# Layer 1's cross-attention with an input shift on GpSimd, scores ahead of a transpose and a mix smoothed by ScalarE, and layer 3's experts in column groups

## The reference, cut to what matters

```python
# L1_xattn
y = jnp.clip(x / scale, -448, 448).astype(bfloat16)    # _div_clamp_fp8, then
y = y.astype(float8_e4m3fn).astype(float32)            # rounded to 8 bits
ln_out = _ln(hidden_states, ln_w, ln_b)
q  = _ln(_fp8_linear_pertensor(ln_out, wq, ...))       # likewise k, qx; v without _ln
core = softmax(q k^T / sqrt(d)) v                      # xout: qx with kx, vx of cond
cat  = concatenate([core, xout])
catq = _div_clamp_fp8(cat, proj_smooth)                # a scale for each column
return (catq @ wproj) * (proj_in_scale * proj_w_scale)
# L3_ffn: 32 experts, at most 32 tokens each, F = 176
g = silu(einsum('ech,ehf->ecf', xe, Wg))
u = einsum('ech,ehf->ecf', xe, Wu)
ye = einsum('ecf,efh->ech', g * u, Wd)
```

## Time and profile before

| what | value |
|---|---|
| time of three runs, us | 3984.92 median, 3978.76 to 3985.75 |
| profiled execution, us | 3986.08, its span 3984.3 |
| PE busy | 3303.0 us, 83% of the span |
| PE weight loads | 2369.1 us, 59% |
| DVE busy | 2550.1 us, 64% |
| ACT busy | 1598.0 us, 40% |
| POOL busy | 301.1 us, 8% |

### The profile page before, as it was taken

How to read it: one execution, slowest core, us unless ns; L and a number is a source line. 1 busy time by engine, 2 the same in 40 slices (tenths; PEclk the granted TensorE clock), 3 DMA queues, 4 the chain that set the end, 5 groups by cost and what they waited for, 6 DMA issues and landing times. The chain is left out here.

```text
span 3984.3 us, 77894 instructions
## 1 busy us (share of the span) xinstructions
PE 3303.0 (83%) x28864; PEld 2369.1 (59%) x28864; DVE 2550.1 (64%) x6580; ACT 1598.0 (40%) x3845; POOL 301.1 (8%) x321
## 2 busy tenths in 40 slices
PE   7899999544687988988989883879977898778899
PEld 6565665211564656656556561658877776645788
DVE  6555555688686777767767767768871487475133
ACT  2244444477243555555555551334332344210011
POOL 3000000000330101101011010001000000000000
PEclk9899999655797999999999995988779999888699
DMA  2000000000400000000000003000000000150100
GB/s 93 29 22 16 22 22 7 1 0 0 144 11 4 1 1 3 1 3 1 1 3 1 1 2 91 1 8 14 16 6 0 1 0 1 36 145 26 39 11 11
DMA packets 89575, 79.10 MB, mean 20 GB/s; under 512 B 16640, under 2 KB 82752, under 8 KB 88896
## 3 DMA queue, kind: packets, MB, share of 16 engines
q1 hardware_dynamic: 88208, 75.57, 6.4%
q10 hardware_dynamic: 1200, 1.11, 0.1%
HBM read 74.57 MB, written 2.10 MB: 19 GB/s over the span
## 5 line engine op out<-in xcount | busy, mean ns | idle before, releaser
L3116 PE MATMUL bank<-L1w_w,L1x_xqT 128*128 128x512 f32 x640 | 303.6, 598 | 2.1 <-DVE L1x_xqT L3360 2.1
L1046 DVE TENSOR_REDUCE L0x_top<-bank 128x4 f32<-128x512 f32 x256 | 159.3, 684 | 105.1 <-PE bank L972 102.0
L1031 ACT ACTIVATE L0x_P<-bank,L0x_level 128x512 f32<-128x512 f32 x256 | 155.1, 688 | 157.1 <-PE bank L992 157.1
L3366 DVE TENSOR_REDUCE L1x_ssq<-L1x_square 128x4 f32<-128x512 f32 x192 | 131.6, 685 | 133.9 <-ACT L1x_square L3243 125.7
L3330 POOL TENSOR_TENSOR L1x_square<-L1x_square,L1x_total 128x512 f32<-128x512 f32 x128 | 133.2, 1041 | 1073.4 <-DVE L1x_total L3395 1073.4
L3265 ACT ACTIVATE L1x_square<-bank,L1x_top 128x128 f32<-128x128 f32 x512 | 182.0, 376 | 19.7 <-DVE L1x_top L3389 19.7
L3177 PE MATMUL bank<-L1w_wp,L1x_catb 128*128 128x256 bf16 x1536 | 188.4, 273 | 0.3 <-DVE L1x_catb L3351 0.3
L3243 ACT ACTIVATE L1x_square<-bank 128x512 f32<-128x512 f32 x192 | 114.9, 599 | 164.4 <-PE bank L3116 164.4
L3116 PEld LDWEIGHTS bank<-L1w_w,L1x_xqT 128*128 128x128 f32 x640 | 115.3, 192 | 99.4 <-issue 91.6
L888 DVE TENSOR_TENSOR x_sb<-x_sb,bank 128x256 f32 (+1 forms) x112 | 47.0, 420 | 197.3 <-PE bank L208 187.5
L3177 PEld LDWEIGHTS bank<-L1w_wp,L1x_catb 128*128 128x128 bf16 x1536 | 150.2, 98 | 35.4 <-issue 17.1
(11 more groups left out here) (650 smaller groups left out, 7915.8 us busy)
## 6 DMA issues: line engine op xcount, KB each, us to landing
L0x_mask<-in_maskrows SPq DMA_DIRECT2D x16, 512.0 KB, 3.3
L3w_wg<-in_L_ffn_Wg SPq DMA_DIRECT2D x8, 704.0 KB, 8.2
L3w_wu<-in_L_ffn_Wu SPq DMA_DIRECT2D x8, 704.0 KB, 9.7
L1a_wp_quarter<-in_L_xattn_wproj SPq DMA_DIRECT2D x4, 1024.0 KB, 6.1
L3x_ctxT<-in_ctxT SPq DMA_DIRECT2D x32, 128.0 KB, 2.1
L3w_wd<-in_L_ffn_Wd SPq DMA_DIRECT2D x8, 512.0 KB, 8.7
L0x_ctxT<-in_ctxT SPq DMA_DIRECT2D x16, 128.0 KB, 2.9
L1w_w<-in_L_xattn_wq SPq DMA_DIRECT2D x1, 2048.0 KB, 10.4
```

The costliest lines, as they stand in the source:

```text
L1031: act.activation(self.P[:, i % 2, r, :], self.work_bank[r][:, :], ACT.Exp, bias=self.level[:, :]).then_inc(self.p_ready.sem, 1)
L1046: dve.tensor_reduce(self.top[:, s, 16 * c + 4 * r:16 * c + 4 * r + 4], self.work_bank[r][:, :].rearrange("p (h k) -> p h k", h=4), X, ALU.max,
L3116: last = pe.matmul(made_bank[n % 4][:, :], inputs(SOURCE[n], k), w[:, k, 4 * n:4 * n + 4, :], start=(k == 0), stop=(k == C - 1))
```

## The change

The input's shift by `lnb` and its product with `in_inv` go from DVE to POOL, and the product `y4` is 16 bits wide. On PE, make_v(3) and score(0) stand ahead of flip(9); on ACT, exponentials(0) stand behind turn_hat(9) and exponentials(1) behind turn_hat(10). DVE's scale_out is gone: ACT's new `smooth_out(m)`, four activations with a scale column from PSUM to 16 bits in `yc`, stands behind the copy of turn_p(m+1), and `quantize(m)` clips `yc` in place. In the experts `hidden` holds the 32 tokens of an expert still in one of four column groups and moves its 352 columns of `Wg` and `Wu`; `turn` transposes the product back; `ye` is copied by DVE.

```diff
@@ L1_xattn, PE
+                pe.wait_ge(v_ready.sem, v_ready.after(b, 1))
+                make_v(3)
+                score(0)
                 flip(NG - 3)
-                score(0)
                 score(1)
                 flip(NG - 2)
                 flip(NG - 1)
-                pe.wait_ge(v_ready.sem, v_ready.after(b, 1))
-                make_v(3)
@@ ACT
+                def smooth_out(m):
+                    act.wait_ge(mixed.sem, mixed.after(b, m + 1))
+                    if m >= 2:
+                        act.wait_ge(cat_ready.sem, cat_ready.after(b, m - 1))
+                    for j in range(4):
+                        last = act.activation(yc[:, (m % 2) * 512 + j * 128:(m % 2) * 512 + (j + 1) * 128], mix_bank[m % 2][:, j * 128:(j + 1) * 128],
+                                              ACT.Copy, scale=smooth[:, 4 * m + j:4 * m + j + 1])
+                    last.then_inc(o_read.sem, 1)
...
                 for m in range(MG):
                     if m + 1 < MG:
                         turn_p(m + 1)
+                    smooth_out(m)
                     if m + 3 < MG:
                         exponentials(m + 3)
@@ POOL
+            def shift_x(b):
+                pool.wait_ge(x_scaled.sem, x_scaled.after(b))
+                step(pool.tensor_tensor(kit.xn[:, :], kit.xn[:, :], lnb[:, :], ALU.add))
+                pool.tensor_tensor(y4, kit.xn[:, :].unsqueeze(1).to_broadcast([128, 4, D]), in_inv[:, :, :],
+                                   ALU.mult).then_inc(y4_ready.sem, 1)
@@ DVE
-                step(dve.tensor_tensor(kit.xn[:, :], kit.xn[:, :], lnb[:, :], ALU.add))
-                step(dve.tensor_tensor(y4, kit.xn[:, :].unsqueeze(1).to_broadcast([128, 4, D]), in_inv[:, :, :], ALU.mult))
...
+                def quantize(m):
+                    smoothed = yc[:, (m % 2) * 512:(m % 2) * 512 + 512]
                     dve.wait_ge(o_read.sem, o_read.after(b, m + 1))
-                    step(dve.tensor_scalar(yc[:, 0:512], cat[:, :], E4M3_TOP, -E4M3_TOP, ALU.min, ALU.max))
+                    step(dve.tensor_scalar(smoothed, smoothed, E4M3_TOP, -E4M3_TOP, ALU.min, ALU.max))
...
                     if m + 1 < MG:
                         invert(m + 1)
-                    scale_out(m)
                     if m + 3 < MG:
                         maxima(m + 3)
@@ L3_ffn, PE
+                    for k in range(C):
+                        for j in range(PER):
+                            at = (g * PER + j) * CAP
+                            last = pe.matmul(hidden_bank[g % 2][j * CAP:(j + 1) * CAP, 0:2 * F], xeT[:, k, at:at + CAP],
+                                             wgu[:, g % SLOTS, j, k, :, :].rearrange("p n f -> p (n f)"),
+                                             start=(k == 0), stop=(k == C - 1), tile_position=(0, j * CAP))
...
+                hidden(0)
+                hidden(1)
+                for g in range(GROUPS):
+                    turn(g)
+                    if g + 2 < GROUPS:
+                        hidden(g + 2)
+                    down(g)
```

More of the change, by code:

```diff
@@ L3286, in batch @@
                 turn_hat(NG - 3)
+                exponentials(0)
                 turn_hat(NG - 2)
-                exponentials(0)
+                exponentials(1)
                 turn_hat(NG - 1)
-                exponentials(1)
                 keep_v(3)
@@ L3325, in _, with share @@
         def _(pool):
-            with pool.Fori(0, B) as b:
+            step = Steps(pool, pool_own)
+            def shift_x(b):
[3 more added lines that the diff above has]
+                                   ALU.mult).then_inc(y4_ready.sem, 1)
+            def share(b, m):
+                pool.wait_ge(inv_ready.sem, inv_ready.after(b, m + 1))
+                rows = P[:, m % 3, :].rearrange("p (h k) -> p h k", h=4)
+                pool.tensor_tensor(rows, rows, total[:, 4 * m:4 * m + 4].unsqueeze(2).to_broadcast([128, 4, 128]),
+                                   ALU.mult).then_inc(shared.sem, 1)
+            step.restart()
+            shift_x(0)
+            with pool.Fori(0, B - 1) as b:
+                step.restart()
+                shift_x(b + 1)
                 for m in range(MG):
[L3328 to L3331, removed]
+                    share(b, m)
+            for m in range(MG):
+                share(B - 1, m)
         @block.vector
@@ L3341, in scale_x, with to_e4m3, from_clipped @@
                     step(norm_vector(kit, dve, b, kit.xn[:, :]))
-                step(dve.scalar_tensor_tensor(kit.xn[:, :], kit.xn[:, :], rms[:, bass.ds(b, 1)], lnw[:, :], ALU.mult, ALU.mult))
-                step(dve.tensor_tensor(kit.xn[:, :], kit.xn[:, :], lnb[:, :], ALU.add))
-                step(dve.tensor_tensor(y4, kit.xn[:, :].unsqueeze(1).to_broadcast([128, 4, D]), in_inv[:, :, :], ALU.mult))
[L3346 to L3351, removed]
+                dve.scalar_tensor_tensor(kit.xn[:, :], kit.xn[:, :], rms[:, bass.ds(b, 1)], lnw[:, :], ALU.mult, ALU.mult).then_inc(x_scaled.sem, 1)
+            def to_e4m3(out, wide, n):
+                step(dve.tensor_scalar(yc[:, 0:n], wide, E4M3_TOP, -E4M3_TOP, ALU.min, ALU.max))
+                return from_clipped(out, yc[:, 0:n], n)
+            def from_clipped(out, clipped, n):
+                power, both = grid[:, 0:n], sums[:, 0:n]
+                step(dve.tensor_scalar(power.bitcast(U16), clipped.bitcast(U16), 0x7F80, None, ALU.bitwise_and))
+                step(dve.tensor_scalar(power.bitcast(U16), power.bitcast(U16), E4M3_LOW_BITS, E4M3_GRID_BITS, ALU.max, ALU.add))
+                step(dve.tensor_tensor(both, clipped, power, ALU.add))
+                return dve.tensor_tensor(out, both, power, ALU.subtract)
             def round_x(b):
-                step(dve.tensor_scalar(yc[:, 0:4 * D], flat(y4), E4M3_TOP, -E4M3_TOP, ALU.min, ALU.max))
-                from_clipped(flat(yb[:, :, :]), 4 * D).then_inc(xq_ready.sem, 1)
+                dve.wait_ge(y4_ready.sem, y4_ready.after(b))
+                to_e4m3(flat(yb[:, :, :]), flat(y4), 4 * D).then_inc(xq_ready.sem, 1)
                 dve.wait_ge(xq_ready.sem, xq_ready.after(b))
@@ L3395, in invert @@
                     dve.reciprocal(part, part).then_inc(inv_ready.sem, 1)
[L3397 to L3400, removed]
+                def quantize(m):
+                    smoothed = yc[:, (m % 2) * 512:(m % 2) * 512 + 512]
                     dve.wait_ge(o_read.sem, o_read.after(b, m + 1))
-                    step(dve.tensor_scalar(yc[:, 0:512], cat[:, :], E4M3_TOP, -E4M3_TOP, ALU.min, ALU.max))
-                def quantize(m):
+                    step(dve.tensor_scalar(smoothed, smoothed, E4M3_TOP, -E4M3_TOP, ALU.min, ALU.max))
                     if m >= 3:
                         dve.wait_ge(left.sem, left.after(b, m - 2))
-                    from_clipped(catb[:, m % 3, :], 512).then_inc(cat_ready.sem, 1)
+                    from_clipped(catb[:, m % 3, :], smoothed, 512).then_inc(cat_ready.sem, 1)
                     dve.wait_ge(cat_ready.sem, cat_ready.after(b, m + 1))
@@ L3487, in L3_ffn @@
         SLOTS = GROUPS - 1
-        wg, wu = (wx.sb(n, [128, SLOTS, PER, C, F]) for n in ("wg", "wu"))
+        wgu = wx.sb("wgu", [128, SLOTS, PER, C, 2, F])
         wd0, wd1 = wx.sb("wd0", [128, SLOTS, PER, D]), wx.sb("wd1", [128, SLOTS, PER, D])
@@ L3674, in hidden, with turn, down @@
                         pe.wait_ge(gu_ready, g - 1)
[L3675 to L3682, removed]
-                    last.then_inc(made, 1)
[L3685 to L3689, removed]
-                    pe.wait_ge(gu_ready, g + 1)
+                    for k in range(C):
[4 more added lines that the diff above has]
+                                             start=(k == 0), stop=(k == C - 1), tile_position=(0, j * CAP))
+                    last.then_inc(made, 1)
+                def turn(g):
+                    pe.wait_ge(gu_ready, g + 1)
+                    if g >= 2:
+                        pe.wait_ge(guT_ready, g - 1)
+                    turn_tensor(kit, pe, turn_bank[g % 2], gu[:, g % 2, :], 2).then_inc(gu_turned, 1)
+                def down(g):
+                    pe.wait_ge(guT_ready, g + 1)
                     if g >= 2:
@@ L3704, in silu @@
                         act.wait_ge(gu_ready, g - 1)
-                    act.activation(act_g[:, g % 2, 0, :], hidden_bank[g % 2][:, 0:128], ACT.Silu)
-                    act.activation(act_g[0:F1, g % 2, 1, :], hidden_bank[g % 2][0:F1, 128:256], ACT.Silu).then_inc(silu_ready, 1)
+                    act.activation(act_g[:, g % 2, :], hidden_bank[g % 2][:, 0:F], ACT.Silu).then_inc(silu_ready, 1)
                 silu(0)
@@ L3711, in _, with multiply @@
                         silu(g + 1)
-                    act.wait_ge(out_made, g + 1)
-                    act.copy(ye[:, g, :], out_bank[g % 2][:, 0:D]).then_inc(out_ready, 1)
+                    act.wait_ge(gu_turned, g + 1)
+                    if g >= 2:
+                        act.wait_ge(out_made, g - 1)
```

(15 more changed lines are left out.)

25 lines of the change are left out of this document (14 added, 11 removed).

## The result

The changed kernel takes 4050.96 us (median of four runs, 4049.22 to 4054.72) against 3982.24 before: ratio 1.0174, 95% interval 1.0156 to 1.0191. It is slower by some 69 us; the forecast was 4045 us. The profiled execution took 4054.72 us.

What follows compares the result with a forecast made beforehand. No engine alone bound cross-attention, with DVE and PE nearly full in the mix loop; PE bound the experts. 3986.1 +116.5 +10.6 −67 = 4046.2, less 1.2 to the median: 4045 us, range 4008 to 4090.

Steps and rivals of the forecast that it cites:

- Circle: Mix loop: invert(m+1), share, turn_p, copy, smooth_out(m), quantize(m), invert(m+2) wait in a ring; turn 3.74 to 5.55 us, +10.9 a batch.
- Scores in front: Batch head: make_v(3) fills PE's wait before flip(9), so turn_x and what follows come earlier, −1.9 us a batch.
- The sum: Whole kernel: 3986.1 us profiled, +116.5 cross-attention, +10.6 clock, −67 experts, giving 4046.2; 1.2 above the median, so 4045.
- Input shift: Batch input: POOL's add and product, 2.7 us, stay hidden before DVE's clip; PE waits less, −0.4 us a batch.
- the first shift: Before the batch loop: the first batch's shift on POOL is not hidden, +1 us once.
- End of the batch: From invert(7) to the next flip(0): late quantizations hide under PE's leftover work, 11.5 us for 12.99, −1.5 a batch.
- Batch without loss on the circle: One cross-attention loop batch before any clock loss: 10.9−1.9−1.5−0.4 = +7.1 us, +106.5 for 15.
- Clock: Mix loop: PE idles about 1.9 us a turn, so its clock may halve on turn_p; +10.6 us taken, bounds 0 and +42.
- the rival: Mix loop: the clock falls in every turn, +42 in place of +10.6 us, 4076 us; chance 0.13.
- the quarter: Mix loop: share taken of the +42 us bound for half clock on turn_p in every turn, +10.6 us.
- Last batch: Final cross-attention batch: no end-of-batch gain, so 10.9−1.9 = +9 us.
- Experts: Layer 3 experts: wide column passes and the clock rising to full take 24.5 us in place of 91.5, −67.

Runs made afterwards that it cites:

- runs 1 and 2: Changed kernel with one move each: smooth_out(m) ahead of the copy of turn_p(m+1) on ACT, 3876.9 us; invert(m+2) ahead of quantize(m) on DVE, 3851.2 us.
- run 3: Changed kernel with the four smoothing activations replaced by one copy, leaving out the column scales: 3985.6 us.
- run 5: Kernel before with only the mix smoothed by ScalarE, at the same queue places as in the change: 4143.6 us, ratio 1.0394.
- run 7: Kernel before with only make_v(3) and score(0) ahead of flip(9) and the exponentials moved accordingly: 3965.1 us, ratio 0.9949.
- run 8: Kernel before with only the input's shift on GpSimd, 16 bits: 3971.8 us, ratio 0.9962.
- Run 6: Kernel before with only the experts in column groups: 3914.2 us, ratio 0.9825.

## Why the prediction was right, step by step

- **Circle.** Right as to mechanism, order and size: 5.61 us a turn for 5.55 predicted. Every link came out within 0.05 us of the row from which it was taken; the four activations took 1.15 us (1.14 taken). My estimate of 1.27 us from the Trainium skill's figures ("ScalarE: Activation LUTs", section on what ACT_TABLE_LOAD costs) is 0.12 more than this trace shows. Cutting either of two links (runs 1 and 2) or shortening one (run 3) moved the time as a circle must. Six turns are 33.95 us for 33.3, 0.06 more in each and 0.28 more in the first (5.89), and against 22.55 before +11.4 a batch, not +10.9. Not foreseen was the first turn: it is the scores in front that lengthen it, as run 5 without them has 5.60.
- **Scores in front.** −2.0 for −1.9 where it was looked for, and flip(9) no longer waits. The sum let everything behind turn_x keep its order and come 1.9 us earlier; it left out that the copy of turn_p(0) then waits for ACT's own queue. That gives back 0.58 a batch alone (run 7) and 0.28 in the changed kernel, whose circle hides the rest. That a half-clock stretch comes to more of the heads with this part alone (12 of 15 instead of 8) was not in the sum either.
- **Input shift.** Hidden as predicted: add and product took 0.73 and 2.36 us on POOL, in place of 0.8, which was an estimate without a row, and the 1.9 of the row; the product ended at 1423.79, the clip began at 1425.58. −0.28 a batch (run 8) for −0.4; the first shift +1.2 for +1.
- **End of the batch.** −1.6 for −1.5 (run 5); from invert(7) to flip(0) 11.39 us for 11.5 predicted (1398.99 to 1410.38).
- **Batch without loss on the circle.** 11.1 (run 5) −2.0 (run 7) −0.28 (run 8) −1.6 (run 5) +0.28 (the first turn, which only the parts together have) = +7.5, and 79.50−71.97 is +7.5, for the +7.1 of the sum.
- **Clock.** Right as to mechanism, in part luck as to size. Stretches at the half clock lengthen the heads of the 15 batches of the loop, from invert(0) to invert(2), by 10.7 us in all; in the kernel before it was 10.2, so nothing is new there. New are 6.2 us in the later turns: where the clock falls on turn_p the turn is up to 6.08 us, 0.46 more, as the rival said of each turn; but that meets single turns. With 1.3 us in the last batch it is some 8 us, for 10.6 predicted; the quarter was a choice, not a reading. The shown turn has leave at half speed (2.64 us for 1.47), and its length is still 5.62: there a low clock off the path cost nothing.
- **Last batch.** From its invert(0) to its last leave 47.87 us for 34.56, +13.3 where the sum has +10.9 (the −1.9 in its +9 lies ahead of that invert(0)): mis-sized by 2.4. Its six turns took 35.29 us, two of them 6.07 and 6.08 with turn_p at half speed.
- **Experts.** 23.2 us for 24.5; a turn was 2.55 for 2.65, and the clock was at the half level only for the first 3.4 us (mean 0.93 over the window of 24 us), so it rose during the hidden projections. The prediction's reading that it rises in the down projections was weak: before, it rose once, behind the fourth of them (3717.2), and not behind the three ahead of it. Run 6 gives the part alone as 70 by the ratio, 74 by the medians.
- **The total.** 4051 is 6 us above 4045. Against the profiled execution, 4054.7 us for the sum's 4046.2, 8.5 are missing: the cross-attention +131.5 for +126.1 (above the 115 to 127 that were named as a sign), the first shift 0.2 more, the unchanged stages +4.1 for nothing, the experts 1.2 less.

## What to carry to other kernels

Before moving work to an engine with time to spare, write down the queue in front of it: an instruction placed behind another that waits for a round trip inherits that wait, and whoever waits for it passes it on. If its result then stands ahead of the instruction that starts the next round trip, a circle is closed, and its length can be summed from single rows of the profile, here to about 1%. Such a loss is mended in the order, not in the work: moving one reciprocal ahead of the rounding turned +69 us into −132, so that the same smoothing on ScalarE is the fastest complete version that was run (3851 us, and 3848 with both moves). And a stretch that comes earlier on one engine gains only as much as the next engine's queue lets through: of the 2.0 us at the head of a batch run 7 kept 1.4.

## What the runs showed of the hardware

GpSimd wrote the 128x1024 product to 16 bits in 2.36 us, where a product of the same shape, of other operands, to 32 bits takes 1.90. And the granted clock at the head of a batch differed between kernels that are small shifts apart: after an idle stretch of PE of about 2.5 us it fell to the half level in 8 of 15 batches before, in 12 with the scores in front alone, and in one with the input shift alone. What tells these apart was not settled.
